# A message-passing kernel: the filter bias moved from VectorE into an accumulation on TensorE

## The chip, the cores and the metric

The kernel runs on one core of a Trainium2 chip. The metric is the device time of one execution in microseconds (us). A core has TensorE (PE in the profile, with PEld for its weight loads), VectorE (DVE), ScalarE (ACT), GpSimd (POOL) and SyncE (SP), each with its own instruction stream; they are ordered against each other by semaphores alone. The on-chip memory is SBUF; TensorE writes to PSUM, which VectorE and ScalarE can read.

## The reference, cut to what matters

Four graph layers over 3125 nodes of 128 features and 53125 edges sorted by destination. The second of them has five convolutions, and the change is in those:

```python
for i in range(DEPTH):                                   # DEPTH = 5
    W = ssp(rbf @ fw1[i] + fb1[i]) @ fw2[i] + fb2[i]     # the filter of every edge
    W = W * C[:, None]
    h = x @ lin1_w[i]
    msg = h[src] * W                                     # the message of every edge
    agg = jax.ops.segment_sum(msg, dst, num_segments=n) / denom
    x = x + ssp(agg) @ lin2_w[i] + lin2_b[i]
    ...                                                  # layer norm
```

`ssp` is softplus minus ln 2. The first, third and fourth graph layers (called the first, gated and count phases here) gather rows and sum them in the same way without a filter.

## The kernel before

**Tiling.** The edges are cut into 52 groups of 1024 (`GROUPS`); a group is 8 chunks of 128 edges and is worked on in two halves `h` of 4 chunks (`HALF`). There are eight phases: first, five convolutions, gated, count. In each, GpSimd gathers the source rows of every group from a table in HBM with 8 indirect DMAs (`gather`, L575) into `rows`, a ring of 10 groups (`RING`). GpSimd's only wait inside a phase is for a free slot of the ring (`staged`, L573), which VectorE gives with the copy of `stage` (L1016) once the rows have been read. A phase's gathers begin after the tables of the phase before are written (`table_ready`).

**A convolution on TensorE** (`conv_edges`, `filters`, `hidden_units`, `message_sums`). In iteration g it issues, in this order: `filters(l, g+1)`, which makes the filter of the next group, per half four products of 128x128 (L713) into one of the two banks `filt_ps`; in even iterations `hidden_units(g//2+1)`, four products over 512 columns (L703), which make the input of softplus for groups g+2 and g+3; steps for nodes whose sums are done (L621, L629, L636); and `message_sums(g)`, eight products of the messages with the scatter matrix (L726). A half of `filters` waits for softplus (`ssp_full`) and for the free bank (`filt_free`).

**On ScalarE** `softplus_logs` turns each of four strips of a pair of groups into its logarithm part with three activations (L874 to L876), in the order 0, 2, 1, 3; strips 0 and 2 belong to the even group.

**On VectorE** (`conv_edges`), in iteration g: `rows_in(g)` waits for the gathered rows (L1020); `messages(g)` multiplies `msg` by `rows`, in two halves (L1212); `stage(g)`; `take_filters(l, g+1)` adds the bias `fb2` to the filter in PSUM and writes it to `msg` of the next group, in two halves (L1205), which frees the PSUM banks; `softplus_rest(g+2)` waits for ScalarE and finishes two strips (L1198); `weighted(g+1)` builds the next scatter matrix (L1006, L1010); `add_sums(g)` waits for `message_sums(g)` and adds the sums into `agg` (L1030). Then come node steps in some iterations: a block of 2 or 3 node tiles (12 blocks) has its mean, value, state, deviation and rows in five consecutive iterations (L1216, L1223, L1228 to L1070, L1053 to L1055, L1239).

So the filter of group g+1 depends on nothing that waits for the rows of group g: VectorE took filter g out of PSUM one iteration earlier.

Of the kernel before, what the change touches and what calls it, by code (L numbers as in the profile page):

```python
# [21 lines left out]
ALU = mybir.AluOpType  # L22
# [3 lines left out]
P = 128  # L26
N_NODES = 3125
N_EDGES = 53125
D = 128
# [11 lines left out]
HALF = CH // 2  # L41
# [22 lines left out]
def build(nc, a, out):  # L64
    ctx = ExitStack()
    with ctx:
# [6 lines left out]
        def sem(name):  # L73
            return ctx.enter_context(nc.semaphore(name))
# [144 lines left out]
        slog_full = sem("slog_full")  # L219
        ssp_full = sem("ssp_full")  # L220
        filt_full = sem("filt_full")
        filt_free = sem("filt_free")
        msg_full = sem("msg_full")
        agg_full = sem("agg_full")
        mean_full = sem("mean_full")
# [20 lines left out]
        def strip(g, h):  # L246
            return 2 * h + g % 2

        def msg_of(g, h):
            return msg[:, g % 2, h, :]  # L250
# [7 lines left out]
        def over_tiles(row, n):  # L258
            return row.unsqueeze(1).broadcast_to([P, n, D])
# [248 lines left out]
        with nc.Block() as block:  # L508
# [77 lines left out]
            def _(pe):  # L586
# [119 lines left out]
                def filters(l, g):  # L706
                    for h in range(2):
                        pe.wait_ge(ssp_full, 1)
                        pe.sem_inc(ssp_full, -1)
                        pe.wait_ge(filt_free, 1)  # L710
                        pe.sem_inc(filt_free, -1)  # L711
                        for c in range(HALF):
                            mm = pe.matmul(filt_ps[h][:, c * D:(c + 1) * D],  # L713
                                           hidden[:, strip(g, h), c * P:(c + 1) * P], fw2[:, l, :], start=True, stop=True)
                        mm.then_inc(filt_full, 1)

                def message_sums(g):
# [215 lines left out]
            def _(dve):  # L933
# [7 lines left out]
                for s in range(RING):  # L941
                    dve.sem_inc(staged[s], 1)
                dve.sem_inc(sum_free, 1)
                dve.sem_inc(filt_free, 2)

                def prepare_weights():

# [250 lines left out]
                        dve.scalar_tensor_tensor(hidden[:, n, :], hid_ps[n], nfb1_l[:, 0:1], hidden[:, n, :],  # L1198
                                                 ALU.max, ALU.add).then_inc(ssp_full, 1)

                def take_filters(l, g):
                    for h in range(2):
                        dve.wait_ge(filt_full, 1)
                        dve.sem_inc(filt_full, -1)  # L1204
                        dve.tensor_tensor(msg_of(g, h).rearrange("p (c d) -> p c d", d=D),  # L1205
                                          filt_ps[h].rearrange("p (c d) -> p c d", d=D),
                                          over_tiles(fb2[:, l, :], HALF), ALU.add).then_inc(filt_free, 1)

                def messages(g):
                    for h in range(2):  # L1210
                        part = msg_of(g, h).rearrange("p (c d) -> p c d", d=D)
                        dve.tensor_tensor(part, part, rows[:, g % RING, h * HALF:(h + 1) * HALF, 0:D], ALU.mult)\  # L1212
                           .then_inc(msg_full, 1)

                def conv_mean(b):
                    dve.tensor_tensor(node_mean[:, 0:size(b) * P], agg[:, block_nodes(b)], deg[:, block_nodes(b)],  # L1216
# [51 lines left out]
                def conv_edges(l, last):  # L1268
                    with dve.Fori(0, n_pass):
                        softplus_rest(0)  # L1270
                        softplus_rest(1)
                        take_filters(l, 0)
                        own(weighted(0, c_e))
                        dve.sem_inc(scatter_full, 1)
                        for g in range(GROUPS + NODE_STEPS):
                            if g < GROUPS:
                                rows_in(g)
                                messages(g)
                                stage(g)
                            if g + 1 < GROUPS:  # L1280
                                take_filters(l, g + 1)
                            if g + 2 < GROUPS:
                                softplus_rest(g + 2)
                            if g + 1 < GROUPS:
                                own(weighted(g + 1, c_e))
                                dve.sem_inc(scatter_full, 1)
                            if g < GROUPS:
                                add_sums(g)
                            for b in due(g, 0, even=True):
                                conv_mean(b)  # L1290
                            for b in due(g - 1, 0, even=True):
                                conv_value(b)
                            for b in due(g - 2, 0, even=True):
                                conv_state(b, last)
                            for b in due(g - 3, 0, even=True):
                                node_deviation(b)
                                if last:
                                    conv_out(b)
                            if last:
                                for b in due(g - 4, 0, even=True):  # L1300
                                    node_deviation(b)
                                    gate_rows(b)
                            else:
                                for b in due(g - 4, 0, even=True):
                                    conv_rows(b, l)
                        if last:
                            dve.wait_ge(score_full, BLOCKS)
                            dve.sem_inc(score_full, -BLOCKS)
                        next_pass()
                    last_sum()  # L1310
# [67 lines left out]
```

## Time and profile before

| | us |
|---|---|
| median of 3 runs (4655.5 to 4660.45) | 4658.06 |
| the profiled execution's own time | 4652.54 |
| its span, first to last instruction | 4650.7 |

| engine | busy us | share of the span | instructions |
|---|---|---|---|
| PE | 2564.6 | 55% | 13213 |
| DVE | 2304.7 | 50% | 4815 |
| ACT | 1316.3 | 28% | 2293 |
| POOL | 3381.1 | 73% | 3337 |

### The profile page before, as it was taken

How to read it: one execution, taken by the hardware profiler on the slowest of the kernel's cores; microseconds unless marked ns; L12 is line 12 of the kernel's file. 1: busy time of each engine (PE TensorE's matmuls, PEld its weight loads, DVE VectorE, ACT ScalarE, POOL GpSimd, SP SyncE). 2: the span in 40 equal slices, each digit the busy share in tenths (PEclk: the TensorE clock that was granted, in tenths of full speed). 3: DMA queues.
4: the chain of work that ended last, by engine and by line, in shares of the span. 5: the costliest groups of instructions: out<-in, count | busy, mean ns of one | idle time of the engine just before them, and what ended most of it. 6: DMA issues, size and time to landing. Idle time of an engine off the chain costs nothing. (4 is left out here: it accounts for less than half of the span.)

```text
span 4650.7 us, 50632 instructions
## 1 busy us (share of the span) xinstructions
PE 2564.6 (55%) x13213; PEld 2299.3 (49%) x13213; DVE 2304.7 (50%) x4815; ACT 1316.3 (28%) x2293; POOL 3381.1 (73%) x3337
## 2 busy tenths in 40 slices
PE   3445466666566665666656676566673333333343
PEld 2444455555465654656546565455562333323333
DVE  4222265665656656566565665666664344321111
ACT  2212144342333433343333433334341111100000
POOL 5777677777677776777767777677773777767776
PEclk9999987776677766777667766666765555555555
DMA  6333222221222222222222222222221222212221
GB/s 136 91 95 96 68 62 64 67 67 49 63 64 68 65 53 62 64 68 65 53 61 64 68 64 55 58 63 66 66 58 25 55 56 56 56 44 56 55 56 53
DMA packets 194085, 297.20 MB, mean 64 GB/s; under 512 B 81758, under 2 KB 116680, under 8 KB 193788
## 3 DMA queue, kind: packets, MB, share of 16 engines
q0 software_dynamic: 106496, 219.17, 18.3%
q10 hardware_dynamic: 33942, 57.75, 4.3%
q1 hardware_dynamic: 53350, 16.87, 1.5%
q8 instruction: 119, 1.95, 0.2%
q14 instruction: 178, 1.46, 0.1%
HBM read 271.98 MB, written 21.57 MB: 63 GB/s over the span
## 5 line engine op out<-in xcount | busy, mean ns | idle before, releaser
L575 POOL DMA_INDIRECT rows<-table,staged_src x3328 | 3380.1, 1016 | 1256.2 <-issue 889.0
L726 PE MATMUL pD<-scatter,msg 128*128 128x80 f32 x4160 | 786.5, 368 | 684.2 <-PEq L724 684.1
L726 PEld LDWEIGHTS pD<-scatter,msg 128*128 128x128 f32 x4160 | 744.3, 277 | 757.8 <-issue 757.6
L665 PE MATMUL pD<-scatter,rows 128*128 128x80 f32 x2496 | 573.1, 424 | 891.1 <-PEq L663 539.7
L665 PEld LDWEIGHTS pD<-scatter,rows 128*128 128x128 f32 x2496 | 544.2, 330 | 922.4 <-issue 922.4
L713 PE MATMUL pC<-fw,hidden 128*128 (+1 forms) x4160 | 843.2, 384 | 171.4 <-PEq L711 170.7
L713 PEld LDWEIGHTS pC<-fw,hidden 128*128 128x128 f32 x4160 | 797.5, 293 | 200.1 <-issue 199.7
L1212 DVE TENSOR_TENSOR msg<-msg,rows 128x512 f32<-128x512 f32 x520 | 336.3, 688 | 478.4 <-DVEq L1020 476.1
L874 ACT ACTIVATE hidden<-pA,fb_l 128x512 f32<-128x512 f32 x260 | 176.5, 679 | 1110.6 <-ACTq L884 1110.6
L1016 DVE COPY staged_src<-src_i 128x8 int32<-128x8 int32 x416 | 75.2, 181 | 727.6 <-DVEq L1024 727.6
L875 ACT ACTIVATE hidden<-hidden 128x512 f32<-128x512 f32 x520 | 327.5, 630 | 64.5 <-ACTq L778 4.0
L876 ACT ACTIVATE hidden<-hidden 128x512 f32<-128x512 f32 x520 | 327.5, 630 | 62.7 <-ACTq L778 1.6
L1205 DVE TENSOR_TENSOR msg<-pC,fb 128x512 f32<-128x512 f32 x520 | 333.2, 681 | 6.7 <-DVEq L1204 6.7
L1006 DVE TENSOR_TENSOR onehot<-win,dst_rel 128x640 bf16<-128x640 f32 x364 | 297.1, 816 | 25.0 <-DVEq L939 25.0
L1030 DVE TENSOR_TENSOR agg<-agg,pD 128x80 f32 x416 | 98.8, 237 | 331.8 <-DVEq L1024 276.9
L1010 DVE TENSOR_TENSOR scatter<-onehot,c_e 128x640 f32<-128x640 bf16 x260 | 214.8, 826 | 38.2
L1198 DVE SCALAR_TENSOR_TENSOR hidden<-pA,nfb_l,hidden 128x512 f32<-128x512 f32 x260 | 192.7, 741 | 58.7 <-DVEq L1197 58.7
L1198 DVE SCALAR_TENSOR_TENSOR hidden<-pB,nfb_l,hidden 128x512 f32<-128x512 f32 x260 | 193.0, 742 | 50.3 <-DVEq L1197 49.0
L703 PE MATMUL pA<-basis,fw_l 32*128 32x512 f32 x520 | 165.4, 711 | 36.2 <-PEq L700 36.2
L1144 DVE TENSOR_TENSOR gate<-score,rows 128x640 f32<-128x640 f32 x52 | 42.9, 825 | 270.5 <-DVEq L1020 270.5
L874 ACT ACTIVATE hidden<-pB,fb_l 128x512 f32<-128x512 f32 x260 | 174.4, 671 | 0.6
L703 PE MATMUL pB<-basis,fw_l 32*128 32x512 f32 x520 | 165.3, 711 | 0.0
(190 smaller groups left out, 1561.2 us busy)
## 6 DMA issues: line engine op xcount, KB each, us to landing
rows<-table,staged_src POOLq DMA_INDIRECT x3328
basis<-basis_d ACTq DMA_DIRECT2D x130, 256.0 KB
table<-node_rows SPq DMA_DIRECT2D x66, 128.0 KB, 1.8
msg<-in_edge_weight_dram ACTq DMA_DIRECT2D x54, 128.0 KB, 3.1
basis_d<-basis ACTq DMA_DIRECT2D x26, 256.0 KB, 3.6
hidden<-in_edge_weight_dram ACTq DMA_DIRECT2D x48, 128.0 KB, 3.4
out_dram<-node_rows SPq DMA_DIRECT2D x12, 128.0 KB, 1.8
table<-node_rows SPq DMA_DIRECT2D x11, 132.0 KB, 2.4
```

The source lines that it names most:

```text
L575: pool.indirect_dma_start(out=rows[:, s, j, 0:width], out_offset=None, in_=tab[:, :], in_offset=bass.IndirectOffsetOnAxis(ap=staged_src[:, ...
L665: mm = pe.matmul(sum_ps, rows[:, g % RING, j, 0:D], scatter[:, g % 2, j, :], start=(j == 0), stop=(j == CH - 1))
L703: pe.matmul(hid_ps[n], fw1_l[at, :], basis[at, t % BASIS_RING, :], start=True, stop=True)\
L713: mm = pe.matmul(filt_ps[h][:, c * D:(c + 1) * D], hidden[:, strip(g, h), c * P:(c + 1) * P], fw2[:, l, :], start=True, stop=True)
L726: mm = pe.matmul(sum_ps, msg_of(g, h)[:, c * D:(c + 1) * D], scatter[:, g % 2, HALF * h + c, :], start=(h == 0 and c == 0), stop=(h == 1 a ...
L874: own(act.activation(dst, arg, ACT.Abs, **bias))
L875: own(act.activation(dst, dst, ACT.Exp, scale=-1.0))
L876: act.activation(dst, dst, ACT.Ln, bias=1.0).then_inc(full, 1)
L1006: return dve.tensor_tensor(dst, over_chunks(win[:, :]), per_chunk(dst_rel, g), ALU.is_equal)
L1198: dve.scalar_tensor_tensor(hidden[:, n, :], hid_ps[n], nfb1_l[:, 0:1], hidden[:, n, :], ALU.max, ALU.add).then_inc(ssp_full, 1)
L1205: dve.tensor_tensor(msg_of(g, h).rearrange("p (c d) -> p c d", d=D), filt_ps[h].rearrange("p (c d) -> p c d", d=D), over_tiles(fb2[:, l, : ...
L1212: dve.tensor_tensor(part, part, rows[:, g % RING, h * HALF:(h + 1) * HALF, 0:D], ALU.mult)\
```

## The change

The bias is laid into PSUM by a product of one row of ones with `fb2` (512 columns, L709 on), which starts an accumulation; the four filter products of the half add to it. VectorE no longer copies the filter out: `take_filters` is gone, and `messages(g)` reads the filter straight from PSUM and multiplies it by the gathered rows. The bank is free once that product is done, so TensorE waits for `msg_full` (h+1 for half h) before it begins the filter of the next group; `filt_free` is gone.

```diff
@@ def filters(l, g), TensorE
                         pe.wait_ge(ssp_full, 1)
                         pe.sem_inc(ssp_full, -1)
-                        pe.wait_ge(filt_free, 1)
-                        pe.sem_inc(filt_free, -1)
+                        if g > 0:
+                            pe.wait_ge(msg_full, h + 1)
+                        pe.matmul(filt_ps[h].rearrange("p (c d) -> p c d", d=D), ones[0:1, :],
+                                  fb2[0:1, l, :].unsqueeze(1).broadcast_to([1, HALF, D]), start=True, stop=False)
                         for c in range(HALF):
                             mm = pe.matmul(filt_ps[h][:, c * D:(c + 1) * D],
-                                           hidden[:, strip(g, h), c * P:(c + 1) * P], fw2[:, l, :], start=True, stop=True)
+                                           hidden[:, strip(g, h), c * P:(c + 1) * P], fw2[:, l, :], start=False, stop=(c == HALF - 1))
                         mm.then_inc(filt_full, 1)
@@ VectorE
-                def take_filters(l, g):
+                def messages(g):
                     for h in range(2):
                         dve.wait_ge(filt_full, 1)
                         dve.sem_inc(filt_full, -1)
                         dve.tensor_tensor(msg_of(g, h).rearrange("p (c d) -> p c d", d=D),
                                           filt_ps[h].rearrange("p (c d) -> p c d", d=D),
-                                          over_tiles(fb2[:, l, :], HALF), ALU.add).then_inc(filt_free, 1)
-
-                def messages(g):
-                    for h in range(2):
-                        part = msg_of(g, h).rearrange("p (c d) -> p c d", d=D)
-                        dve.tensor_tensor(part, part, rows[:, g % RING, h * HALF:(h + 1) * HALF, 0:D], ALU.mult)\
-                           .then_inc(msg_full, 1)
+                                          rows[:, g % RING, h * HALF:(h + 1) * HALF, 0:D], ALU.mult).then_inc(msg_full, 1)
@@ conv_edges, VectorE
                         softplus_rest(0)
                         softplus_rest(1)
-                        take_filters(l, 0)
@@ -1277,8 +1270,6 @@
-                            if g + 1 < GROUPS:
-                                take_filters(l, g + 1)
```

## Rows read from the trace of the kernel before

**Rows 1.** The page's costliest groups: GpSimd's gathers; busy, mean ns, idle before.

```profile
L575 POOL DMA_INDIRECT rows<-table,staged_src x3328 | 3380.1, 1016 | 1256.2 <-issue 889.0
```

**Rows 2.** Timeline of GpSimd where the second convolution begins: start, us, [idle before].

```profile
1176.73 2.99 POOL L575 DMA_INDIRECT rows<-table,staged_src  x1 [23.08 <-POOLq L573]
```

**Rows 3.** Windows: gathers of the second and fifth convolution and the count phase.

```profile
1176.73:1737.58 560.85, 365.04 (x1962) 323.86 (x1962) 345.51 (x662) 214.71 (x375) 434.37 (x416) 0.70 0.24 64
...
2926.25:3486.54 560.29, 370.23 (x1897) 326.93 (x1898) 367.63 (x758) 222.98 (x420) 433.80 (x416) 0.69 0.24 64
...
4114.52:4637.90 523.38, 197.61 (x860) 187.28 (x860) 72.48 (x170) 0.00 (x0) 396.90 (x416) 0.50 0.21 55
```

**Rows 4.** Timeline of all engines, one even iteration in mid-layer.

```profile
1400.39 1.29 DVE L1212 TENSOR_TENSOR msg<-msg,rows 128x512 f32<-128x512 f32 x2 [1.58 <-DVEq L1020]
1401.23 3.67 PE L726 MATMUL pD<-scatter,msg 128*128 128x80 f32 x16 [5.17 <-PEq L724]
...
1404.70 3.70 PE L713 MATMUL pC<-fw,hidden 128*128 x16
...
1408.33 0.89 PE L703 MATMUL pA<-basis,fw_l 32*128 32x512 f32 x1
...
1411.87 1.29 DVE L1212 TENSOR_TENSOR msg<-msg,rows 128x512 f32<-128x512 f32 x2 [3.83 <-DVEq L1020]
```

**Rows 5.** Timeline of TensorE and VectorE, first iteration of the second convolution.

```profile
1198.40 6.47 PE L713 MATMUL pC<-fw,hidden 128*128 x32 [17.81 <-PEq L711]
1204.81 0.69 PE L703 MATMUL pA<-basis,fw_l 32*128 32x512 f32 x1
...
1210.45 0.75 DVE L1198 SCALAR_TENSOR_TENSOR hidden<-pB,nfb_l,hidden 128x512 f32<-128x512 f32 x1 [1.32 <-DVEq L1197]
...
1214.95 1.33 DVE L1212 TENSOR_TENSOR msg<-msg,rows 128x512 f32<-128x512 f32 x2 [0.35 <-DVEq L1020]
```

**Rows 6.** Timeline of TensorE at full clock: sums, then a group's filter.

```profile
1433.02 1.98 PE L726 MATMUL pD<-scatter,msg 128*128 128x80 f32 x16 [1.85 <-PEq L724]
1435.70 2.02 PE L713 MATMUL pC<-fw,hidden 128*128 x16 [0.70 <-PEq L711]
```

**Rows 7.** Windows over single TensorE runs: length, PE, PEld, DVE, ACT, POOL, PEclk, DMA.

```profile
1401.23:1408.33 7.10, 7.10 (x32) 6.88 (x32) 5.26 (x10) 0.00 (x0) 5.34 (x5) 0.50 0.17 46
1429.39:1430.52 1.13, 1.13 (x10) 0.37 (x9) 0.16 (x1) 0.00 (x0) 0.94 (x1) 1.00 0.27 58
1433.02:1437.72 4.70, 4.00 (x32) 3.69 (x32) 4.55 (x8) 4.11 (x8) 3.55 (x4) 1.00 0.24 54
1178.51:1180.60 2.09, 2.09 (x8) 0.51 (x8) 1.94 (x5) 0.00 (x0) 1.79 (x2) 0.50 0.88 321
```

**Rows 8.** Timeline: sums to `agg`; the second convolution's first and last message.

```profile
1156.17 3.67 PE L726 MATMUL pD<-scatter,msg 128*128 128x80 f32 x16 [3.04 <-PEq L724]
...
1160.69 0.24 DVE L1030 TENSOR_TENSOR agg<-agg,pD 128x80 f32 x1 [3.99 <-DVEq L1024]
...
1205.08 1.30 DVE L1212 TENSOR_TENSOR msg<-msg,rows 128x512 f32<-128x512 f32 x2 [0.35 <-DVEq L939]
...
1739.31 1.29 DVE L1212 TENSOR_TENSOR msg<-msg,rows 128x512 f32<-128x512 f32 x2 [1.74 <-DVEq L1020]
```

**Rows 9.** Timeline of VectorE: node steps after `add_sums` (value, state, deviation).

```profile
1407.62 0.42 DVE L1223 SCALAR_TENSOR_TENSOR node_mean<-node_mean,node_log 128x256 f32<-128x256 f32 x1 [0.36 <-DVEq L1221]
...
1419.10 0.42 DVE L1228 TENSOR_TENSOR x<-pD,y 128x256 f32<-128x256 f32 x1 [0.35 <-DVEq L1042]
...
1420.79 0.25 DVE L1070 TENSOR_SCALAR var<-mv 128x2 f32<-128x2 f32 x1
...
1428.78 0.16 DVE L1053 SCALAR_TENSOR_TENSOR newton<-rstd 128x2 f32<-128x2 f32 x1 [0.36 <-DVEq L1051]
```

**Rows 10.** Timeline: a VectorE product of two SBUF tiles, and the gather beside it.

```profile
1179.25 3.49 DVE L1343 TENSOR_TENSOR y<-x,mv 128x3200 f32<-128x3200 f32 x1
...
1180.02 3.53 POOL L575 DMA_INDIRECT rows<-table,staged_src  x1 [0.30 <-POOLq L573]
```

More of the change, by code:

```diff
@@ L221, in build @@
         filt_full = sem("filt_full")
-        filt_free = sem("filt_free")
         msg_full = sem("msg_full")
@@ L943, in _ @@
                 dve.sem_inc(sum_free, 1)
-                dve.sem_inc(filt_free, 2)
                 def prepare_weights():
```

## The prediction, made before the result was known

> **What bounds the kernel now.** I read the page's costliest groups first. GpSimd is the busiest engine: 3328 gathers of 1016 ns, and of its 1256 us of idle time 889 are the 0.3 us between one gather and the next [rows 1]. The other 367 are waits, and the timeline of GpSimd shows where: not inside a phase but between phases, as the 23.08 us before the second convolution [rows 2]. So inside a phase the gathers run without a stop, and the ring of ten groups is never full. By windows a convolution's 416 gathers take 560.85 us, 10.8 us a group, while the count phase's take 523.38, 10.1 a group [rows 3]. The timeline of an iteration agrees from the other side: VectorE stands 3.83 us in the wait for rows before its message, 11.5 us after the one before [rows 4]. All other engines follow the gathers, and TensorE and VectorE have room.
>
> What has to be seen is why they can follow. The filter (L713, 1404.70) and the hidden units (L703, 1408.33) of an even iteration run before the next rows are there and before message 1411.87 [rows 4]: TensorE makes filter g+1 while VectorE waits for rows g. The loop through TensorE, ScalarE and VectorE is laid over two iterations.
>
> **The change part by part.** VectorE loses the two L1205 of each group. They lie in an engine that waits for rows, so they give back nothing by themselves. The message product reads PSUM in place of SBUF; two products over 256 columns, L1228 which reads PSUM and L1223 which doesn't, both last 0.42 us [rows 9], so nothing there.
>
> TensorE gets 520 one-row products over 512 columns. No such product is in the trace; the nearest is a set of four hidden-unit products over 512 columns, which run side by side on different rows of the array: the whole set takes 1.13 us at granted clock 1.00 and 2.09 at 0.50 [rows 7]. Each product is two records; the first of such a set lasts 0.69 [rows 5], so the second adds 1.13 - 0.69 = 0.44, and one product in a stream of others costs twice that, 0.88, or 1.74 at half clock. I take these; the ends of the range are 0.44 (one record's worth, if one row is cheaper) and the whole set. A group's filter without bias is 2.02 us at clock 1.00 [rows 6] and 3.70 at 0.50 [rows 4], by the granted clocks of those windows [rows 7]. With two bias products, F is 3.78 (fast) or 7.18 (slow).
>
> **The new wait is the part that decides.** Filter g+1 may begin only when message g is done, and message g needs rows g and stands behind `add_sums(g-1)` on VectorE. Behind the waiting filter on TensorE stand, in order, the hidden units, the node products and `message_sums(g)`. Who waits for these: ScalarE for the hidden units, then VectorE's `softplus_rest(g+2)` for ScalarE, and behind that on VectorE `weighted(g+1)`, `add_sums(g)` and message g+1. What was laid over two iterations is now one chain per iteration:
>
> Even iteration: message g to TensorE's first product, 0.84 us (1400.39 to 1401.23) [rows 4]; F; then from the hidden units to the next message. That last piece stands in the trace just so, in the first iteration of a layer, where nothing was prepared: L703 at 1204.81, ScalarE's strips, the second L1198 at 1210.45 after a wait, scatter matrix, `add_sums`, next message at 1214.95: 10.14 us [rows 5].
>
> Odd iteration (no hidden units; its strips are ready): 0.84; F; sums of 1.98 (fast) [rows 6] or 3.67 (slow) [rows 4]; from the sums' end at 1159.84 to L1030 at 1160.69, 0.85 [rows 8]; L1030 and the step to the next message, 0.24 + 0.35. VectorE's own work in it is shorter and hidden.
>
> **The clock.** The mean granted clock in the layer is 0.70 [rows 3]. After 17.81 us of idle the 32 records of two filters took 6.47 us [rows 5], where twice the values above would be 4.04 fast and 7.4 slow: slow for about the first 4.8 us of the run (6.47 less 4.04, doubled), fast after. TensorE will now idle once in every iteration: from the sums' end to the next first product, some 2.3 us in the odd one, and some 8 in the even one, where it waits for ScalarE and VectorE. The odd iteration therefore starts slow for 4.8 us: F = 3.78 + 2.4 = 6.2, sums fast. The even one I take slow for 3.7 us, the length of a slow run of sums [rows 4]: F = 3.78 + 1.85 = 5.6. So even: 0.84 + 5.6 + 10.14 = 16.6 us; odd: 0.84 + 6.2 + 1.98 + 1.44 = 10.5 us.
>
> The Trainium skill, "TensorE: Matmul & The Clock Gate", section on HAM oscillation, describes bursts divided by waits that start at half clock each time, which goes against a change that adds a wait to TensorE; the row with 6.47 us agrees with it. The sum uses the row's length only.
>
> **Node steps** come after `add_sums` on VectorE and before the next message, so they lie on the chain, where before they hid in the wait for rows. A block's value step takes 0.36 + 0.42 = 0.78 us, its state step 2.29 (from 0.35 before 1419.10 to 1421.04), its deviation 1.14 (0.36 and three of 0.16 with 0.15 between) [rows 9]; mean and rows I estimate at 1.2 like these. Together 5.4, for 11 blocks within the loop 59 us a layer.
>
> **The sum.** From the first to the last message of a layer there are 51 intervals: 25 even ones with hidden units, and 26 priced as odd. 25 x 16.6 + 26 x 10.5 = 688, with node steps 747 us. Before it was 1739.31 - 1205.08 = 534.2 [rows 8]. What lies before the first and after the last message (the softplus of groups 0 and 1, the last blocks' node steps, the table) is as before: the first message loses L1205 and gains two bias products, some 1 to 3 us either way. So +213 us a layer, five times: +1064. The fifth layer has 22 us more of VectorE work (367.63 against 345.51 busy) [rows 3], all node steps and now on the chain: +22. The profiled execution's 4652.5 + 1086 = 5738.5; it was 5.5 below the median, so I give **5744 us**.
>
> Its own range comes from the clock and the bias. Fast throughout: even 14.8, odd 8.0, so 25 x 14.8 + 26 x 8.0 + 59 = 637, +103 a layer, in all about 5190. Slow throughout: even 0.84 + 7.18 + 10.14 and some 0.9 for the slow hidden units, 19.1; odd 0.84 + 7.18 + 3.67 + 1.44 = 13.1; 878 in all, +343 a layer, about 6400. A bias product at half the price takes 0.44 to 0.87, twice in 51 intervals, off each layer, some 60 us, so 300 in all; at the whole set's price it adds 0.25 to 0.35 each, some 150.
>
> **Rivals.**
> 1. *Slow clock throughout*, 6400 us. The products of one row might not count as work, and they divide F into short pieces; the first, gated and count phases have a clock of 0.50 for whole stretches (count phase) with TensorE busy 38% [rows 3]. Against it: each iteration now has a run of 6 to 9 us without a gap. 12%.
> 2. *Fast clock nearly throughout*, 5190 us. TensorE has more work per message. Against it: the 8 us of idle in each pair of iterations. 10%.
> 3. *The gathers stay the bound*, faster than before. The place is GpSimd: the gather that meets a VectorE product of two SBUF tiles lasts 3.53 us [rows 10] where the mean is 1.02, and ends 0.81 after the product (1182.74 to 1183.55). L1212 is such a product before, and isn't after, since one operand is in PSUM. Price: a convolution's gathers take 560.85 - 523.38 = 37 us more than the count phase's [rows 3]; over five layers at most 187 of gain, and as the scatter products (L1006, L1010) and the long ones at a layer's start remain, I take 40: 4618 us. It decides if a pair of iterations takes less than two groups of gathers, 21.5 us. My fast chain with node steps is 22.8 + 2.3, so even then it doesn't get there; only a bias product near nothing and a shorter way through ScalarE would. 5%.
>    The Trainium skill, "SBUF — State Buffer", section on who interferes with whom, says that a VectorE instruction with two SBUF inputs contends with a GpSimd instruction that reads SBUF; this row agrees. It also infers that descriptor generation isn't held up by such a product, by which there would be nothing to gain here: 4658.
> 4. *No difference*: the ring of ten groups lends 100 us a layer, but to the gathers alone. The table of the next layer needs the last message, so a lag of the loop is paid at the end of every layer. I can see no way to this outcome but rival 3 with its gain lost. 2%.
>
> The forecast's mechanism with a mixed clock keeps 71%. The range should take most of rivals 1 and 2's neighbourhood: **5300 to 6200**. Beyond 0.2%, about what a measurement of this kernel can tell from no change: slower 0.93, within 0.02, faster 0.05.
>
> **What would show it.** After: long waits of GpSimd in L573 inside the layers, with the gathers of a layer some 200 us longer; VectorE's wait for rows (L1020) gone, and in its place waits for softplus (L1197 before) in even iterations and for sums or the filter in odd ones; L1212's successor alternating between some 16 and 10 us; a bias group of 1040 records of 0.5 to 1.2 us; TensorE's wait for `msg_full` long. The first, gated and count phases keep their lengths. Wrong would be: messages that still wait for rows (then the loop keeps up), hidden units that start before the message of their iteration, or intervals of even and odd iterations alike.

## The result and the profile after

The changed kernel took 6459.7 us, median of 4 runs (6456.78 to 6459.96); the kernel before, with one more run, 4656.78 (4 runs). The ratio is 1.3875, its 95% interval 1.3851 to 1.3899: 1803 us slower. The forecast was 5744 us, and its range ended at 6200. The direction and the chain of waits held; the clock that the forecast let TensorE have inside that chain didn't, and with it the size.

The page of the kernel after, its busy times and its costliest groups (busy, mean ns | idle before, what ended most of it):

```profile
PE 3875.9 (60%) x14253; PEld 2712.9 (42%) x14253; DVE 1995.2 (31%) x4295; ACT 1319.8 (20%) x2293; POOL 3255.7 (50%) x3337
...
L574 POOL DMA_INDIRECT rows<-table,staged_src x3328 | 3254.7, 978 | 3185.8 <-POOLq L572 2280.6
L711 PE MATMUL pC<-fb,ones 1*128 (+1 forms) x1040 | 1072.9, 1133 | 1432.6 <-DVE msg L1205 1354.6
```

The gathers are a little shorter than before in the mean (978 ns against 1016 [rows 1]), and GpSimd's idle time has grown from 1256 to 3186 us. Of that, 2281 lie in its wait for a free slot of the ring (L572), in which it stood between the phases alone before: inside a convolution it now waits 228 to 296 us there, and gathers no longer bound the convolutions. TensorE is busy for 1311 us more than before and yet waits for 1355 us, for the message at the head of `filters`. It is neither full nor free: it works and waits in turn with VectorE. The waits on VectorE's side are the other half of that chain (total us, count, longest):

```profile
DVE hidden L1198 <- DVEq L1197: 1685.4, 256, 15.8
DVE agg L1030 <- DVEq L1024: 1223.0, 253, 14.9
```

Softplus (L1197) is waited for twice in each even iteration, once for each strip, and the sums (L1024) in nearly every group; the wait for rows, which stood before each message in [rows 4], is gone from the convolutions.

The timeline of all engines, an even iteration in mid-layer and the start and end of the odd one behind it (start, us, [idle before and what ended it]):

```profile
2010.35 1.29 DVE L1205 TENSOR_TENSOR msg<-pC,rows 128x512 f32<-128x512 f32 x2 [0.37 <-DVEq L1204]
2011.09 2.07 PE L711 MATMUL pC<-fb,ones 1*128 x2 [3.35 <-DVE msg L1205]
2013.09 2.08 PE L714 MATMUL pC<-fw,hidden 128*128 x8
2015.10 2.07 PE L711 MATMUL pC<-fb,ones 1*128 x2
2017.10 2.08 PE L714 MATMUL pC<-fw,hidden 128*128 x8
2019.10 1.22 PE L702 MATMUL pA<-basis,fw_l 32*128 32x512 f32 x1
...
2023.63 0.75 DVE L1198 SCALAR_TENSOR_TENSOR hidden<-pA,nfb_l,hidden 128x512 f32<-128x512 f32 x1 [11.92 <-DVEq L1197]
2025.70 0.75 DVE L1198 SCALAR_TENSOR_TENSOR hidden<-pB,nfb_l,hidden 128x512 f32<-128x512 f32 x1 [1.32 <-DVEq L1197]
...
2030.55 1.28 DVE L1205 TENSOR_TENSOR msg<-pC,rows 128x512 f32<-128x512 f32 x2
2031.28 2.07 PE L711 MATMUL pC<-fb,ones 1*128 x2 [7.71 <-DVE msg L1205]
...
2039.16 3.05 PE L727 MATMUL pD<-scatter,msg 128*128 128x80 f32 x16
...
2043.06 0.24 DVE L1030 TENSOR_TENSOR agg<-agg,pD 128x80 f32 x1 [8.14 <-DVEq L1024]
...
2043.99 1.28 DVE L1205 TENSOR_TENSOR msg<-pC,rows 128x512 f32<-128x512 f32 x2
```

Message to message: 20.20 us over the even iteration, 13.44 over the odd one (20.7 and 14.2 in the mean of the second convolution, node steps included). The even interval is the chain of the prediction: message (2010.35), 0.74 us later the first product, the filter until 2019.10, the hidden units, ScalarE's strips, L1198, the next message. In the odd one TensorE goes from the filter to the sums without a stop.

The granted clock over the first filter, over the run of sums behind it and over the count phase (windows: length, PE, PEld, DVE, ACT, POOL, PEclk, DMA share, GB/s):

```profile
2011.09:2019.10 8.01, 8.01 (x20) 4.55 (x20) 0.62 (x2) 0.00 (x0) 5.08 (x6) 0.50 0.13 33
2021.66:2023.57 1.91, 1.91 (x18) 1.76 (x16) 0.00 (x0) 1.68 (x4) 0.52 (x1) 1.00 0.22 58
...
5918.51:6442.12 523.61, 197.62 (x860) 187.28 (x860) 72.86 (x170) 0.00 (x0) 397.14 (x416) 0.50 0.21 55
```

Eight microseconds of TensorE without a gap run at 1.2 GHz from end to end, and the 1.91 us of sums that start 2.56 us behind them run at 2.4 GHz. The last row is the count phase, 523.61 us against 523.38 [rows 3]: where nothing was changed, nothing moved. The gated phase, not changed either, took 531.6 us where it had taken 536.4; what moves it comes out of the last experiments.

### The profile page after: what moved, and what is told of

The parts are those of the page before. It is cut to its first block and busy times, and to the rows that moved or that the text cites. A ratio compares the mean times of both kernels' runs of the same rounds, so it can differ in the third digit from the quotient of the medians.

```text
span 6455.0 us, 51671 instructions
## 1 busy us (share of the span) xinstructions
PE 3875.9 (60%) x14253; PEld 2712.9 (42%) x14253; DVE 1995.2 (31%) x4295; ACT 1319.8 (20%) x2293; POOL 3255.7 (50%) x3337
## 5 line engine op out<-in xcount | busy, mean ns | idle before, releaser
L574 POOL DMA_INDIRECT rows<-table,staged_src x3328 | 3254.7, 978 | 3185.8 <-POOLq L572 2280.6
L711 PE MATMUL pC<-fb,ones 1*128 (+1 forms) x1040 | 1072.9, 1133 | 1432.6 <-DVE msg L1205 1354.6
L714 PEld LDWEIGHTS pC<-fw,hidden 128*128 128x128 f32 x4160 | 926.2, 327 | 780.9 <-issue 780.9
L714 PE MATMUL pC<-fw,hidden 128*128 (+1 forms) x4160 | 1079.5, 441 | 0.0
L711 PEld LDWEIGHTS pC<-fb,ones 1*128 1x128 f32 x1040 | 255.6, 304 | 1543.1 <-DVE msg L1205 1397.8
L727 PEld LDWEIGHTS pD<-scatter,msg 128*128 128x128 f32 x4160 | 727.8, 271 | 62.8 <-issue 62.8
L727 PE MATMUL pD<-scatter,msg 128*128 128x80 f32 x4160 | 731.4, 352 | 12.9 <-PEq L725 12.9
L1198 DVE SCALAR_TENSOR_TENSOR hidden<-pA,nfb_l,hidden 128x512 f32<-128x512 f32 x260 | 194.2, 747 | 1517.8 <-DVEq L1197 1517.8
L1205 DVE TENSOR_TENSOR msg<-pC,rows 128x512 f32<-128x512 f32 x520 | 334.3, 683 | 56.3 <-DVEq L1204 50.1
L1006 DVE TENSOR_TENSOR onehot<-win,dst_rel 128x640 bf16<-128x640 f32 x364 | 297.3, 817 | 24.5 <-DVEq L940 24.5
L702 PE MATMUL pA<-basis,fw_l 32*128 32x512 f32 x520 | 263.8, 1109 | 36.1 <-PEq L699 36.1
L702 PE MATMUL pB<-basis,fw_l 32*128 32x512 f32 x520 | 263.6, 1109 | 0.0
L1198 DVE SCALAR_TENSOR_TENSOR hidden<-pB,nfb_l,hidden 128x512 f32<-128x512 f32 x260 | 193.8, 745 | 167.6 <-DVEq L1197 167.6
L1010 DVE TENSOR_TENSOR scatter<-onehot,c_e 128x640 f32<-128x640 bf16 x260 | 214.5, 825 | 39.6 <-DVEq L940 2.0
```

The source lines that it names most:

```text
L574: pool.indirect_dma_start(out=rows[:, s, j, 0:width], out_offset=None, in_=tab[:, :], in_offset=bass.IndirectOffsetOnAxis(ap=staged_src[:, ...
L702: pe.matmul(hid_ps[n], fw1_l[at, :], basis[at, t % BASIS_RING, :], start=True, stop=True)\
L711: pe.matmul(filt_ps[h].rearrange("p (c d) -> p c d", d=D), ones[0:1, :], fb2[0:1, l, :].unsqueeze(1).broadcast_to([1, HALF, D]), start=Tru ...
L714: mm = pe.matmul(filt_ps[h][:, c * D:(c + 1) * D], hidden[:, strip(g, h), c * P:(c + 1) * P], fw2[:, l, :], start=False, stop=(c == HALF - 1))
L727: mm = pe.matmul(sum_ps, msg_of(g, h)[:, c * D:(c + 1) * D], scatter[:, g % 2, HALF * h + c, :], start=(h == 0 and c == 0), stop=(h == 1 a ...
L1006: return dve.tensor_tensor(dst, over_chunks(win[:, :]), per_chunk(dst_rel, g), ALU.is_equal)
```

## The experiments

Two theories of the missing 716 us stood against each other. A: the one-row product keeps the clock down, and the clock is what was mis-sized. B: the chain of waits itself, or a dearer product, is longer than worked out, and the clock doesn't come back in this rhythm whatever the product looks like.

**The bias product over all 128 rows.** `inv` holds 1/128 everywhere, and all partitions of `fb2` hold the same bias, so the sum is the bias again. Instructions, waits and columns stay the same in number, but for one instruction at the start that fills `inv`.

```diff
-pe.matmul(filt_ps[h]..., ones[0:1, :],
-          fb2[0:1, l, :].unsqueeze(1).broadcast_to([1, HALF, D]), start=True, stop=False)
+pe.matmul(filt_ps[h]..., inv[:, :],
+          fb2[:, l, :].unsqueeze(1).broadcast_to([P, HALF, D]), start=True, stop=False)
```

> The changed kernel, but the bias product uses all 128 rows of the array: a stationary tile of 1/128 against all 128 copies of the bias, the same length and the same result. Theory A (a product of one row does not keep TensorE's clock up, so the filter of every group runs slow): a filter with bias falls from 8.0 us to between 5.6 and 6.2 as in the prediction, the intervals between messages from 20.4 and 14.1 us to about 17.8 and 11.7 with node steps, and the time to 5700 to 5900. Theory B (the idle time before each run of products makes it slow, whatever the products are): nothing changes, 6460.

It took 5515.7 us, a ratio of 1.1833 (1.177 to 1.1896): 944 us less than with one row. Timeline and window of one group's filter, then the page's groups:

```profile
1607.51 2.08 PE L713 MATMUL pC<-fb,inv 128*128 x2 [3.37 <-DVE msg L1207]
1609.38 1.53 PE L716 MATMUL pC<-fw,hidden 128*128 x8
1610.74 1.02 PE L713 MATMUL pC<-fb,inv 128*128 x2
1611.61 1.05 PE L716 MATMUL pC<-fw,hidden 128*128 x8
```

```profile
1607.51:1612.66 5.15, 5.15 (x24) 3.52 (x24) 0.62 (x2) 0.00 (x0) 3.93 (x5) 0.72 0.18 51
```

```profile
L713 PE MATMUL pC<-fb,inv 128*128 (+1 forms) x1040 | 831.3, 893 | 1503.3 <-DVE msg L1207 1424.1
```

The first product takes 2.08 us, as in the kernel after; within the filter products the clock rises, and the second half takes 1.0 + 1.05. So the wait ahead of the run is the same (3.37 against 3.35 us) and the start is slow in both; only with 128 rows does the clock come back inside the run. Theory B can't give this. The 5700 to 5900 of theory A was missed as well, by 184 us downwards; the section on the prediction says by which terms.

**How many rows, and does it matter what is in them?** The same with 32 rows of 1/32, and with 128 rows of which the stationary holds 1 in the first and 0 in all others.

```diff
+dve.memset(inv[:, :], 1.0 / RADIAL)       # 32 rows
-ones[0:1, :],   fb2[0:1, l, :]...
+inv[0:RADIAL, :], fb2[0:RADIAL, l, :]...
```

```diff
+dve.memset(inv[:, :], 0.0)                # 128 rows, one of them 1
+dve.memset(inv[0:1, :], 1.0)
```

> The changed kernel with the bias product over 32 rows (a stationary tile of 1/32), a quarter of the array. If what keeps the clock is the number of rows at work and a quarter is too few: filter with bias 8.0 us and 6460, as with one row. If anything above a single row will do: 5516, as with 128. Between: the share counts.

> The changed kernel with the bias product over all 128 rows, but with a stationary tile that is 1 in row 0 and 0 in the 127 others: the rows are addressed and stream the bias, and multiply it by zero. If the rows addressed count for the clock: 5516, as with 1/128 in all rows. If the values multiplied count: 6460, as with one row.

One run each: 6467.6 and 5525.3 us. The page's bias group, 32 rows first, 128 rows with 127 of them zero second:

```profile
L713 PE MATMUL pC<-fb,inv 32*128 (+1 forms) x1040 | 1074.6, 1134 | 1442.9 <-DVE msg L1207 1363.2
```

```profile
L714 PE MATMUL pC<-fb,inv 128*128 (+1 forms) x1040 | 838.8, 901 | 1507.5 <-DVE msg L1208 1427.6
```

32 rows behave as one (1134 ns a record against 1133), and 128 rows of which 127 add nothing behave as 128 full ones (901 against 893). Between these runs it is the rows that the instruction spans that make the difference, not what the stationary holds in them. (The moving operand, the bias, was the same in all the rows of both; with zeros there nothing was run.) The Trainium skill, "TensorE: Matmul & The Clock Gate", section on HAM oscillation, puts slow bursts down to the waits between them. The waits here are alike in both kernels, and one of them recovers within the burst: for this case the rule is not the whole of it, and the measurement decides.

**The wait alone.** The bias is left out altogether (the output lacks `fb2`), the filter starts its own accumulation, and VectorE still reads it from PSUM.

```diff
-pe.matmul(filt_ps[h]..., ones[0:1, :], fb2[0:1, l, :]..., start=True, stop=False)
-    hidden[...], fw2[:, l, :], start=False, stop=(c == HALF - 1))
+    hidden[...], fw2[:, l, :], start=True, stop=True)
```

> The changed kernel without the bias product; it leaves the filter bias out. What remains is the new wait of the filter for the message. If the wait is the cause and the product only lengthens it: the filter takes 3.7 us at the slow clock, even intervals 0.84 + 3.7 + 10.3 + 1.15 = 16.0, odd 0.84 + 3.7 + 2 to 3.6 + 1.45 + 1.15 = 9.1 to 10.7, but never under the 10.0 of the gathers, so some 5250. If the product is the whole cause and the wait costs nothing: 4620 to 4660.

5206.7 us, ratio 1.117 (1.1111 to 1.123): the wait costs 549 us without any product. The timeline, one even interval:

```profile
1503.70 1.28 DVE L1203 TENSOR_TENSOR msg<-pC,rows 128x512 f32<-128x512 f32 x2
1504.43 3.78 PE L712 MATMUL pC<-fw,hidden 128*128 x16 [2.89 <-DVE msg L1203]
...
1520.75 1.29 DVE L1203 TENSOR_TENSOR msg<-pC,rows 128x512 f32<-128x512 f32 x2
```

In most groups a run of 3.78 us is over before the clock has risen, so F, the time of a group's filter on TensorE, is 3.7 here in the mean, its slow value. The layer took 635.9 us from first to last message, 102 more than the 534.2 before [rows 8].

**The product alone.** The kernel before, with the one-row product, and VectorE copying the filter out of PSUM where it had added the bias. No new wait on TensorE.

```diff
+pe.matmul(filt_ps[h]..., ones[0:1, :], fb2[0:1, l, :]..., start=True, stop=False)
-    hidden[...], fw2[:, l, :], start=True, stop=True)
+    hidden[...], fw2[:, l, :], start=False, stop=(c == HALF - 1))
@@ take_filters
-dve.tensor_tensor(msg_of(g, h)..., filt_ps[h]..., over_tiles(fb2[:, l, :], HALF), ALU.add)
+dve.tensor_copy(msg_of(g, h), filt_ps[h])
```

> The kernel before with the bias product on TensorE and VectorE copying the filter out of PSUM as before: the product alone, without the new wait. Theory A: TensorE stays slow and needs 8.0 (filter with bias) + 1.05 (hidden units) + 3.6 (sums) + 0.5 (nodes) = 13.2 us a group, more than the 10.8 of the gathers, so 52 x 2.4 = 125 us more a layer, about 5280. Theory B: TensorE is busy nearly all the time, its clock goes up, it needs 7 to 9 us a group and the gathers stay the bound: 4640 to 4670.

> The kernel before with the bias product over 128 rows on TensorE and VectorE copying the filter out as before: the product without the new wait and without the low clock. If the 470 us that the one-row product cost in that place were the clock: TensorE needs some 8 us a group, less than the gathers' 10.8, and the time is 4650 to 4720. If they were the length of the product: 5000 to 5130.

With one row 5126.2 us, ratio 1.0997 (1.0946 to 1.1049); with 128 rows 4665.2, ratio 1.0009 (0.9998 to 1.0021). The page's groups, one row first:

```profile
L712 PE MATMUL pC<-fb,ones 1*128 (+1 forms) x1040 | 909.1, 968 | 168.6 <-PEq L711 167.8
```

```profile
L577 POOL DMA_INDIRECT rows<-table,staged_src x3328 | 3386.6, 1018 | 1261.1 <-issue 889.2
...
L714 PE MATMUL pC<-fb,inv 128*128 (+1 forms) x1040 | 734.8, 796 | 229.6 <-PEq L713 224.5
```

The one-row product costs 468 us in a kernel where TensorE hardly stands still ahead of it (169 us of idle). A group's filter takes 4.3 to 8.1 us, 7.0 in the mean, between its fast and its slow price, and with sums and hidden units it fills the time of a group: TensorE becomes the bound, at about 12 us a group, 618 to 627 in the first four layers. The same work in 128 rows costs nothing that these runs can tell, since TensorE has room for it, and GpSimd is as busy as before (3386.6 us, idle 1261.1, against 3380.1 and 1256.2 [rows 1]). I had expected some 5280 for the first; the clock was down from end to end in 149 of 255 filters, fewer than I had allowed for.

**Where the parts stand.** Added to 4658: product alone +468, wait alone +549, both +1802; with 128 rows +2 (against 4663.1, the kernel before on the same chip; the interval takes in no change), +549 and +858. With one row the whole costs 785 more than its parts added up, since a slow run of 8.0 us now lies in a chain where everybody waits for it. With 128 rows it still costs 307 more than its parts: a product that is free beside the gathers isn't free inside the chain.

**A shorter way through ScalarE.** Strips 0 and 2 of the hidden units are issued ahead of the filter's wait for the message, strips 1 and 3 after the sums; the one-row product stays.

```diff
@@ filters: after both waits for ssp_full, before the first msg_full
+if g % 2 == 1 and g // 2 + 1 < PAIRS:
+    hidden_units(g // 2 + 1, (0, 2))
@@ conv_edges, TensorE
-    if g % 2 == 0 and g // 2 + 1 < PAIRS:
-        hidden_units(g // 2 + 1)
     ...
     message_sums(g)
+    if g % 2 == 0 and g // 2 + 1 < PAIRS:
+        hidden_units(g // 2 + 1, (1, 3))
```

> The changed kernel with two of the four hidden-unit products (strips 0 and 2) issued before the filter's wait for the message, the other two after the sums; nothing else moves. If the stretch of ScalarE behind the hidden units is what makes the even intervals long (20.4 us against 14.1), the even ones fall to about 15, 5.4 us less in 25 intervals of 5 layers: 6460 - 680 = 5780. If the even intervals are long for another reason: 6460 within 50.

5773.4 us, ratio 1.2386 (1.2348 to 1.2423), 686 less than the kernel after. The timeline, one even interval:

```profile
1713.81 1.29 DVE L1209 TENSOR_TENSOR msg<-pC,rows 128x512 f32<-128x512 f32 x2
1715.08 0.74 DVE L1202 SCALAR_TENSOR_TENSOR hidden<-pA,nfb_l,hidden 128x512 f32<-128x512 f32 x1
...
1728.98 1.29 DVE L1209 TENSOR_TENSOR msg<-pC,rows 128x512 f32<-128x512 f32 x2 [0.37 <-DVEq L1208]
```

The strip (L1202) is ready at the message's end where VectorE waited 11.9 us for it, and this even interval is 15.2 us long. So in the kernel after, ScalarE's way lies on the chain behind the slow filter, as the prediction had it.

**Both repairs at once: no new wait at all.** The chain exists only because `filters(l, g+1)` stands ahead of `message_sums(g)`. Put behind the sums, which need the message anyway, it needs no wait of its own; strips 0 and 2 go ahead, 1 and 3 behind, and the product has 128 rows.

```diff
@@ conv_edges, TensorE, iteration g
-    filters(l, g + 1)
-    hidden_units(g // 2 + 1)              # even g
+    hidden_units(g // 2 + 1, (0, 2))      # even g
     ...
     message_sums(g)
+    filters(l, g + 1)                     # without the wait for msg_full
+    hidden_units(g // 2 + 1, (1, 3))      # even g
```

> The fused message with 128 rows in the bias product, hidden units of strips 0 and 2 ahead of the message, then the sums of group g, then the filter of group g+1, then strips 1 and 3. If the chain of waits is as told, a group takes 1.5 (both messages and the step to TensorE) + 2.0 to 3.6 (sums) + 5 to 6 (filter) + 0.2 = 9 to 11 us, close to the 10.0 of undisturbed gathers, and VectorE's sums and node steps lie beside it: 4620 to 4900. If ScalarE still stands in the chain: above 5200.

4617.6 us, ratio 0.9897 (0.9857 to 0.9937): faster than both kernels, by 1% against the one before. Its timeline in mid-layer, and the windows of the second convolution's gathers and of the gated phase, the last row that of the kernel before:

```profile
1405.30 1.29 DVE L1208 TENSOR_TENSOR msg<-pC,rows 128x512 f32<-128x512 f32 x2
1406.13 3.67 PE L728 MATMUL pD<-scatter,msg 128*128 128x80 f32 x16 [1.66 <-PEq L726]
...
1415.04 1.29 DVE L1208 TENSOR_TENSOR msg<-pC,rows 128x512 f32<-128x512 f32 x2 [2.93 <-DVEq L1207]
```

```profile
1163.05:1709.50 546.45, 428.92 (x2170) 314.40 (x2170) 287.95 (x558) 215.89 (x378) 419.95 (x416) 0.82 0.22 65
...
3499.74:4051.87 552.13, 191.85 (x838) 180.55 (x838) 216.65 (x442) 79.16 (x118) 425.64 (x416) 0.50 0.21 54
...
3554.71:4091.14 536.43, 191.90 (x838) 180.50 (x838) 216.76 (x442) 79.16 (x118) 409.96 (x416) 0.50 0.24 55
```

Messages come 9.74 us apart here, and the mean clock of the layer is 0.82. GpSimd is the bound again in the first four convolutions, and a convolution's gathers are shorter than before: 546.45 us against 560.85 [rows 3]. That is the place of the prediction's rival 3, with 14 us a layer. But the gated phase, in which nothing was edited, grew by 16 us (552.13 against 536.43), and the gap ahead of it from 68.2 to 83.1. By the windows of all phases the convolutions give 72 us back, the gap, the gated phase and the first take 32; the span is 39 shorter.

**What a gather waits for.** In the kernel before, an undisturbed gather takes 0.94 us. Each longer one, but for the first of a phase, ends 0.81 us after the end of a VectorE product of two SBUF tiles, one that had begun before the gather and was still running some 0.13 us after the gather's start. (The first gather of a phase meets the memset of `agg`, L991, and the copies behind it: 2.99 us in [rows 2], 4.40 in the gated phase.) Here L1010, `scatter`, holds one (timeline of the kernel before):

```profile
1405.15 0.82 DVE L1010 TENSOR_TENSOR scatter<-onehot,c_e 128x640 f32<-128x640 bf16 x1
1405.30 1.49 POOL L575 DMA_INDIRECT rows<-table,staged_src  x1 [0.30 <-issue]
```

The product ends at 1405.97, the gather at 1406.79. Stretched so by over 0.1 us are 41 us of gathers in a convolution of the kernel before: about 20 by L1010, in 38 of 52 groups, 6 by L1212, 2 by L1006, 12 by the long products at a layer's start. Products with one operand in PSUM never stretched any. The start decides sharply. In the traces of the kernel before, both kernels with the sums first, the 128-row product alone and the run below, of 1071 gathers with a product of two SBUF tiles of 0.6 us or more that had begun over 0.08 us ahead of them and ran on for over 0.3 us, 1068 were held; of 2099 whose product began between 0.02 us ahead of them and 0.30 us behind, 5. If that is right, the product's place in time matters, and one instruction more, put ahead of it, should make the kernel faster. In the kernel before, a small statistics instruction on a tile of ones goes between L1006 and L1010 of the convolutions:

```diff
     own(match(onehot[:, g % 2, :, :], g))
+    own(dve.bn_stats(idle6[:, :], ones[:, :]))
     return dve.tensor_tensor(scatter[...], onehot[...], per_chunk(weights, g), ALU.mult)
```

> The kernel before with one short VectorE instruction (statistics of a constant tile, some 0.3 us) between L1006 and L1010 of a convolution's weighted(), nothing else. L1010 has two SBUF inputs and in the trace of before meets the start of a gather in most groups, which then lasts 1.49 us in place of 0.94. If a gather is held only where it starts inside such a product, moving L1010 by 0.45 us puts it between two starts: up to 17 us less a layer, 4570 to 4600. If the hold depends on the amount of VectorE work and not on its place: 4658 or more.

4619.6 us, ratio 0.9916 (0.99 to 0.9933), with 260 instructions more. Timeline, and windows of the second and fifth convolution and the gated phase:

```profile
1406.09 0.29 DVE L1012 BATCH_NORM_STATS2 idle<-ones 128x6 f32<-128x128 f32 x1
1406.25 0.94 POOL L576 DMA_INDIRECT rows<-table,staged_src  x1 [0.30 <-issue]
1406.53 0.82 DVE L1013 TENSOR_TENSOR scatter<-onehot,c_e 128x640 f32<-128x640 bf16 x1
```

```profile
1163.09:1706.46 543.37, 347.87 (x1962) 304.32 (x1962) 362.02 (x713) 214.64 (x375) 416.89 (x416) 0.73 0.23 66
2863.39:3423.47 560.08, 365.15 (x1848) 322.20 (x1848) 369.90 (x772) 219.93 (x411) 433.60 (x416) 0.68 0.22 64
3507.99:4057.36 549.37, 192.08 (x838) 180.55 (x838) 216.83 (x442) 79.16 (x118) 422.87 (x416) 0.50 0.21 54
```

The same product, 0.28 us behind the gather's start instead of 0.15 ahead of it, holds nothing. The second convolution's gathers take 543.37 us instead of 560.85, and L1010's share of the stretch falls from 20 to 4 us. My 4570 to 4600 was missed by 20 us, since the fifth convolution gained nothing, the gap behind it grew by 16, and the gated phase, in which nothing was touched, lost 13: its own product (L1155) now met a gather's start in 41 to 43 of 52 groups instead of 20.

That too can be tried by moving it. The same instruction, ahead of L1155, in the kernel with the sums first:

```diff
 part = scatter[:, g % 2, :, :]
+own(dve.bn_stats(idle6[:, :], ones[:, :]))
 dve.tensor_tensor(part, part, now, ALU.mult).then_inc(scatter_full, 1)
```

> The kernel with the sums first (fused message, 128 rows, 4618 us), and in the gated phase one short VectorE instruction before L1155's successor, which multiplies two SBUF tiles and meets the start of a gather in 43 of 52 groups there. If the hold depends on the place, the gated phase falls from 552 us to about 530, and the time to 4595; if on the amount of work, it stays at 4618 or rises.

4596.4 us, ratio 0.9864 (0.9847 to 0.988), the lowest of all. Its interval and that of the kernel with the sums first overlap, and the two ran on different chips; what carries the reading is the phase itself, in the two traces. The gated phase's window:

```profile
3499.28:4024.68 525.40, 191.60 (x837) 180.31 (x838) 229.82 (x493) 79.05 (x118) 398.97 (x416) 0.50 0.23 56
```

The gated phase falls from 552.13 to 525.40 us, and GpSimd's busy time in it from 425.64 to 398.97, next to the 396.90 of the count phase [rows 3], in which hardly any gather is held. Gathers held by L1155's successor fall from 43 to 2.

The gap after the fifth convolution grew by 15 to 18 us in all three of these kernels. The traces show where it lies. In the kernel before, the last message of the second convolution starts 1.7 us after the end of its last gather, that of the fifth 27.4 us after it; in these three kernels it is 44 to 45 us in the fifth. So in the fifth convolution the ring lets the gathers run ahead of a loop that is slower than they are, and shorter gathers alone can't shorten that layer. What makes that loop still slower in these kernels wasn't tried.

## Why the prediction was wrong: the chain was right, the clock in it wasn't

**What bounds the kernel, and the new wait: right.** The chain of each iteration is the one that was written down. A layer goes from 534 to 885 us between its first and last message (timeline of the kernel after, first and last message of the second and of the fifth convolution):

```profile
1557.21 0.69 DVE L1205 TENSOR_TENSOR msg<-pC,rows 128x512 f32<-128x512 f32 x1 [0.84 <-DVEq L1204]
...
2441.93 1.29 DVE L1205 TENSOR_TENSOR msg<-pC,rows 128x512 f32<-128x512 f32 x2
...
4353.37 0.69 DVE L1205 TENSOR_TENSOR msg<-pC,rows 128x512 f32<-128x512 f32 x1 [0.66 <-DVEq L1204]
...
5323.33 1.29 DVE L1205 TENSOR_TENSOR msg<-pC,rows 128x512 f32<-128x512 f32 x2
```

**The step that failed is "The clock".** It let the clock come back inside a filter, after 3.7 or 4.8 us, from a row of products that all span the array [rows 5]. The new filter has a one-row product ahead of each half, and with it the clock stays at 0.50 from end to end in 236 of the 255 filter runs, and none of the others is shorter than 7.7 us. The prediction had named this as rival 1, with 12% and 6400 us, and argued against it by the 6 to 9 us without a gap. The argument was wrong: 8.01 us without a gap ran slow. The 128-row run shows the cause, not only its size. It also shows that the miss is smaller than the step: the clock was worth 944 us, and the other terms were 228 us too high together, which by luck brought the forecast nearer.

By term, for an ordinary layer, with the means of the second convolution in the trace of the kernel after:

| term | forecast us | measured us | difference a layer |
|---|---|---|---|
| message to TensorE | 0.84 | 0.74 | -5 (51 intervals) |
| F, even iteration | 5.6 | 8.09 | +62 (25) |
| F, odd iteration | 6.2 | 8.07 | +49 (26) |
| sums, odd iteration | 1.98 | 3.19 | +31 (26) |
| from the hidden units (even) or the sums (odd) to the next message, node steps included | 350 a layer | 352 a layer | +2 |
| first to last message | 747 | 884.7 | +138 |

The differences account for the 138. That the fifth term comes out is luck: it was too low by about 0.9 us in each even iteration, for hidden units at the slow clock, and too high in the node steps, which have a length of 59.0 us as forecast but run in part beside the wait ahead of the next message. The first four layers grew by 354.8, 350.5, 351.4 and 351.5 us where 213 were forecast, which is 557 of the miss of 718 us between the profiled executions (6456.78 - 5738.5).

**The bias product** was taken at 1.74 us at half clock; it takes 2.0, within the bound of the whole set, and with four filter products of 2.0 a half is 4.0 where the slow price was 3.59: F is 8.0 to 8.1 and not 7.18, 46 us a layer. Rival 1, with 878 a layer, is within 7 us of the 884.7 all the same, because it took the sums (3.67) and the node steps too high. Its 6400 in all came out 60 us low mostly by the fifth layer.

**The fifth layer** is 970.0 us, 85 more than the others; I had added 22. Its node steps are 109 us instead of 59, so 50. Another 30 lie on ScalarE, which the prediction had left out: in nine even iterations its gate steps (L814, L820) stand ahead of the strips (timeline of ScalarE in the kernel after, hidden units at 4539.66):

```profile
4542.83 0.26 ACT L814 ACTIVATE node_rows<-pD,gate_b 128x2 f32<-128x2 f32 x1 [16.01 <-ACTq L813]
4544.73 0.38 ACT L820 ACTIVATE score<-pD 128x256 f32<-128x256 f32 x1 [1.64 <-ACTq L819]
4545.45 0.69 ACT L875 ACTIVATE hidden<-pA,fb_l 128x512 f32<-128x512 f32 x1 [0.33 <-ACTq L885]
```

The first strip starts 5.8 us after the hidden units instead of 2.2; over the layer these steps add up to 84.1 us instead of 53.6. Some 5 us I haven't placed. There was also an error of the sum: the layer before was already 24 us longer than the others (558.4), and to add the same increase counts that twice. Net, the fifth layer is 177 of the miss; what lies outside first and last messages takes 16 off, and 557 + 177 - 16 is the 718.

**Rival 2, the fast clock throughout**: the 128-row run is nearest to it, and shows what the mixed clock does when it does come back. F is 5.07 in even iterations and 5.80 in odd ones, where 5.6 and 6.2 were forecast; intervals with node steps 16.7 and 10.6, where the forecast comes to 17.8 and 11.7; a layer 693.7 instead of 747; 5516 us instead of 5744. Of the 53 us a layer, 24 are F (25 x 0.53 + 26 x 0.40) and 29 the other terms, 21 of them the stretch with the node steps. So with the clock's return as forecast the sum was still 4% high, and so was my expectation of 5700 to 5900 for that run.

**Rival 3, the gathers stay the bound**, 4618 us: not in the kernel as changed, whose loop never keeps up. In the kernel with the sums first it is what happened. That 4617.6 was measured there is coincidence, for it comes by another sum than mine, 72 us gained in the convolutions and 32 lost elsewhere. L1212 was a small part of it (6 of 41 us a layer); what the change moved was the place of L1010, whose holds fell from about 20 to 4 us in the second convolution, while those of L1006 rose from 3 to 11. The Trainium skill, "SBUF — State Buffer", section on who interferes with whom, says that a VectorE instruction with two SBUF inputs contends with a GpSimd instruction that reads SBUF, which the 1.49 us beside L1010 bear out, if the gather counts as one: it takes its indices from `staged_src` in SBUF. Its inference that such a product leaves descriptor generation alone can't be carried over to these gathers, which last up to 3.53 us beside one [rows 10]. Whether reading the indices or making the descriptors is what is held, no run here tells.

**What bounds the kernel before** was read from the second convolution. In the fifth the loop already ran 27 us behind the gathers.

**What would show it**: waits in the gathers inside the layers, softplus and sums in alternation, 1040 bias records of 1133 ns, TensorE's wait for the message and the first and count phases at their old length all came; the gated phase was 5 us shorter. Intervals were 20 and 14 us, not 16 and 10, and the gathers of a convolution took 194 to 263 us longer.

## What to carry to other kernels

A bias or another small operand that TensorE brings into an accumulation, in a kernel whose clock isn't up all the time, is worth trying over all 128 rows, with 1/128 or zeros in the stationary: it costs the same records, and here it was worth 944 us. Before an operation is fused onto an accumulator, ask who now holds the bank and until when; the consumer's wait becomes the producer's, and it is free only where the producer's next work stands behind something that waits for that consumer anyway. Where GpSimd's gathers bound a phase, look at which VectorE products of two SBUF tiles run across the start of a gather, in the phases behind the edit too, and whether the loop behind the gathers keeps up with them in every phase.

## What the hardware did that I had not expected

- A product that spans 1 or 32 of the 128 rows, ahead of four full ones, leaves the clock at 1.2 GHz over runs of 8.01 us; spanning 128 rows it lets it rise in the same place, 127 of them multiplied by zero included (6460 and 6468 us against 5516 and 5525).
- A gather that starts inside a product of two SBUF tiles ends 0.81 us after the product (1405.97 to 1406.79). Started 0.28 us ahead of the product it takes its usual 0.94 us. A shift by some 0.4 us is worth 17 us in a convolution of 52 groups, and 260 idle instructions made the kernel 0.8% faster.
- A phase's length can change by 13 to 16 us with nothing edited in it: the gated phase took 536.4 us before, 531.6 in the kernel after, 552.1 and 549.4 in the two kernels above and, with its product moved, 525.4.
- The granted clock on record can be wrong for a stretch. For the first phase it reads 1.00 in the kernel before and 0.52 in the 128-row run, but sixteen records of sums take 3.67 us in both (starting at 300.27 and 301.35 us), which is the slow price of [rows 4]. The mean of 0.688 for the kernel before holds that stretch. Beside a clock belongs the time of a product.
